# A fused decoder layer: first turn's last outputs after all of m, the query weights' high part on ScalarE, the last down products behind the first scores

## The reference, cut to what matters

```python
def attn(x, w_qkv, w_swiglu, w_out):            # x is a layernorm of the input, 8 x 256 x 512
    q, k, v = split(rms(x) @ w_qkv.T, 3)
    q, k = rms(q), rms(k)
    w = exp(k)
    kv_cum, w_cum = cumsum(w * v, 1), cumsum(w, 1)
    y = sigmoid(q) * (kv_cum / (w_cum + 1e-06))
    u, g = split(y @ w_swiglu.T, 2)              # 2 x 2048 columns
    return x + u * silu(g) @ w_out.T             # m = u * silu(g), "down" = m @ w_out.T
x = x + attn(layernorm(x), ...)
x = x + cross_attention(layernorm(x), ctx, mask, w_q, w_k, w_v, w_o, b_o)   # 32 heads of 16, 8 groups, causal
x = x + ffn(layernorm(x), ...)                   # 8 experts, top 2, and a shared one
```

## Time and profile before

| | us |
|---|---|
| median of 3 runs (1362.88 to 1364.53) | 1363.5 |
| the profiled execution | 1360.16 |
| its span, first to last instruction | 1358.4 |
| PE busy | 1298.8 (96%) |
| PEld busy | 1033.3 (76%) |
| DVE busy | 875.4 (64%) |
| ACT busy | 725.6 (53%) |
| POOL busy | 739.1 (54%) |

### The profile page before, as it was taken

The page is one execution under the profiler, slowest core; times in us unless marked ns, Lnnn a source line. Parts: engine busy times, 40 slices in busy tenths (PEclk is TensorE's granted clock), DMA queues, the critical chain, the costliest instruction groups (busy, mean ns, idle before and its releaser), DMA issues.

```text
span 1358.4 us, 23793 instructions
## 1 busy us (share of the span) xinstructions
PE 1298.8 (96%) x7988; PEld 1033.3 (76%) x7988; DVE 875.4 (64%) x2182; ACT 725.6 (53%) x1305; POOL 739.1 (54%) x722
## 2 busy tenths in 40 slices
PE   8999997999999999999989999999989999999994
PEld 6888776888888888888877777777767977666672
DVE  5888755444556744445658788778786586666661
ACT  4444444444345444434328777777775325777772
POOL 4557676456657754566556556445553113656562
PEclk9999998999999999999999999999999999999997
DMA  6000011111112111111220000000012914555553
GB/s 232 1 1 1 16 32 62 47 47 47 47 47 77 64 47 48 47 47 47 96 91 21 2 21 21 21 21 5 3 48 89 393 52 149 102 97 108 100 99 42
DMA packets 30152, 86.21 MB, mean 63 GB/s; under 512 B 2960, under 2 KB 7824, under 8 KB 28624
## 3 DMA queue, kind: packets, MB, share of 16 engines
q1 hardware_dynamic: 19856, 59.51, 12.4%
q0 software_dynamic: 10176, 25.17, 9.4%
HBM read 65.54 MB, written 19.14 MB: 62 GB/s over the span
## 4 chain that ended last, share of the span: by engine, by line
PE 76%; DVE 6%; POOL 6%; ACT 5%; issue 4%; DMA 1%; POOLq 0%; DVEq 0%; ACTq 0%
PE ps L974 12%; PE ps L976 11%; PE ps L975 11%; PE ps L1091 7%; PE ps L1093 6%; PE ps L1092 6%; PE ps L1249 5%; PE ps L1430 5%; PE ps L1241 2%; DVE den L1914 2%; ACT sc L1744 2%; PE ps L1341 2%; PE ps L1273 2%; PE ps L1267 1%; ACT pt L1732 1%
## 5 line engine op out<-in xcount | busy, mean ns | idle before, releaser
L770 POOL TENSOR_TENSOR w_up<-w_up_raw,w_up 128x512 fp32r<-128x512 f32 x120 | 134.2, 1162 | 89.2 <-ACT w_up L1575 89.2
L2088 DVE TENSOR_TENSOR acc<-ps,acc 128x512 f32<-128x512 f32 x128 | 88.0, 688 | 124.6 <-PE ps L976 123.9
L2219 DVE CUSTOM_DVE_ANT_0 sc<-ps,msk 128x256 f32<-128x256 f32 (+1 forms) x512 | 146.3, 353 | 26.6 <-PE ps L1241 15.2
L1732 ACT COPY pt<-ps 128x512 f32<-128x512 f32 x192 | 111.6, 581 | 77.4 <-PE ps L1249 77.4
L948 POOL DMA_INDIRECT out<-yx,ids x39 | 77.0, 1974 | 82.0 <-DMA out<-yx,ids 53.5
L1249 PEld LDWEIGHTS ps<-ident,sc 128*128 128x128 f32 x768 | 83.6, 140 | 45.0 <-issue 24.0
L1744 ACT ACTIVATE sc<-sc,mxs 128x256 f32<-128x256 f32 x256 | 116.8, 508 | 1.3 <-DVE mxs L2219 0.9
L866 POOL TENSOR_TENSOR sc<-mxs,sc 128x512 f32<-128x512 f32 x64 | 64.6, 1042 | 92.9 <-DVE mxs L2219 92.9
L1249 PE MATMUL ps<-ident,sc 128*128 128x128 f32 x768 | 109.7, 279 | 3.7 <-ACT pt L1732 3.7
L1091 PE MATMUL ps<-yt,w_up 128*128 128x512 f32 x256 | 99.9, 390 | 2.1 <-ACT ups__93 L1625 1.4
L974 PE MATMUL ps<-w_dn,m_s 128*128 128x512 f32 x256 | 99.7, 390 | 0.7 <-DVE acc L2088 0.7
(11 more groups left out here) (332 smaller groups left out, 3664.8 us busy)
## 6 DMA issues: line engine op xcount, KB each, us to landing
rawx<-weights SPq DMA_DIRECT2D x8, 1536.0 KB, 12.9
w_up_raw<-weights SPq DMA_DIRECT2D x15, 768.0 KB, 4.4
w_dn_raw<-weights SPq DMA_DIRECT2D x16, 512.0 KB, 5.3
wlow<-weights SPq DMA_DIRECT2D x3, 1536.0 KB, 6.4
ctx_raw<-ctx_t SPq DMA_DIRECT2D x8, 512.0 KB, 4.8
h_rows<-hd POOLq DMA_DIRECT2D x16, 256.0 KB, 4.8
out<-acc SPq DMA_DIRECT2D x4, 1024.0 KB, 4.7
w_up_raw<-weights SPq DMA_DIRECT2D x15, 256.0 KB, 4.7
```

The costliest lines, as they stand in the source:

```text
L770: ins = nc.gpsimd.tensor_tensor(out=to[:, j, 1, two, :, :].rearrange("p o k n -> p (o k n)"), in0=raw[:, j, 1, two, :].rearrange("p o n -> ...
L1732: nc.scalar.copy(pt[:, u % PLACES, :], bank).then_inc(turned[k], 1)
L2088: nc.vector.tensor_tensor(acc[:, tile, :], ps[:, BANK_D[t % 2], :], acc[:, tile, :], ALU.add).then_inc(mlp["acc"], 1)
L2219: ins = nc.vector.tensor_tensor_reduce(sc[:, at_, n * w:(n + 1) * w], ps[:, u % 4, n * w:(n + 1) * w], m_in, -0.25, 3e38, ALU.add, ALU.min ...
```

## The change

It touches three places. (1) In the first turn `y_a(7, 1)` goes from the middle of DVE's list to its end, behind both lows of chunk 1; low(0,0,0) goes ahead of the second up_2; in turn 1 PE's downs 0 and 1 go behind p6, together with the wait for y_a(7, 1). For this batch the denominators are made in place in `yraw`, whose place is free a little later than that of `wce_last` (wait for three steps of the first weights' split in place of one). (2) In turn 15 ACT makes the hi of the query weights, between silu_1 and p7_copy, in place of POOL; and POOL issues the zero rows in its turn 1, not ahead of `ctx_split(0)`. (3) Downs 6 and 7 of turn 15 go behind the scores of set 0, and down 5 behind the queries; DVE makes the mask and h_c of batch 1 ahead of reading the queries; DVE and PE both wait for the last down's sum behind it.

```diff
-        def wce_of(b):
-            return wce_last[:, :] if b + 1 == BATCH else wce[:, :]
+        def wce_of(b, half):
+            return yraw[:, b % PAIRED, half, :] if b + 1 == BATCH else wce[:, :]
+        def den_of(b, half):
+            return yraw[:, b % PAIRED, half, :] if b + 1 == BATCH else den[:, :]
...
 POOL, split_slot
-                own.link(nc.gpsimd.tensor_copy(wsplit[:, p, 0, :], wlow[:, p, 1, :]))
+                if name == "x":
+                    pool.wait_ge(c["x_hi"], 1)
+                else:
+                    own.link(nc.gpsimd.tensor_copy(wsplit[:, p, 0, :], wlow[:, p, 1, :]))
...
                 split_dn(u)
+                if u == 1:
+                    zero_rows()        # the two DMA issues of line 834, which go from behind this loop
...
 PE, turns 1 to 15
-                if u == 1:
-                    pe.wait_ge(a["y"], 2 * BATCH)
-                down(u - 1, 0)
+                if u > 1:
+                    down(u - 1, 0)
                 p7(u, 0)
                 p7(u, 1)
-                down(u - 1, 1)
+                if u > 1:
+                    down(u - 1, 1)
                 p6(u, 0)
                 p6(u, 1)
+                if u == 1:
+                    pe.wait_ge(a["y"], 2 * BATCH)
+                    down(0, 0)
+                    down(0, 1)
                 down(u - 1, 2)
...
 PE, behind values
-            for t in range(PIECES - 2):
+            for t in range(PIECES - 3):
                 down(TURNS - 1, t)
             pe.wait_ge(c["hT"], TPB)
             for half in range(2):
                 queries(half, ps[:, 2 + half, :])
-            for t in range(PIECES - 2, PIECES):
-                down(TURNS - 1, t)
+            down(TURNS - 1, PIECES - 3)
...
 PE, pass_c, behind scores(b, u // 4)
+                    if b == 0 and u == 0:
+                        down(TURNS - 1, PIECES - 2)
+                        down(TURNS - 1, PIECES - 1)
+                        pe.wait_ge(mlp["acc"], PIECES * TURNS)
...
 ACT, w_cum and the turns
-                    act.wait_ge(mlp["w_up"], 1)
-                nc.scalar.activation(wce_of(b), ps[:, 5, :], ACT.Copy, bias=1e-6).then_inc(a["wce"], 1)
+                    act.wait_ge(mlp["w_up"], 3)
+                nc.scalar.activation(wce_of(b, half), ps[:, 5, :], ACT.Copy, bias=1e-6).then_inc(a["wce"], 1)
...
+                if u + 1 == TURNS:
+                    act.wait_ge(raw_slot["x"], 32)
+                    nc.scalar.copy(wsplit[:, 0, 0, :], wlow[:, 0, 1, :]).then_inc(c["x_hi"], 1)
                 if u > 0:
                     p7_copy(u, 0)
...
 DVE, turn 0
             up_2(0, 0)
-            up_2(0, 1)
             up_1(0, 0)
             hidden_1(0, 0)
+            low(0, 0, 0)
+            up_2(0, 1)
             up_1(0, 1)
             hidden_1(0, 1)
-            low(0, 0, 0)
             low(0, 1, 0)
-            y_a(BATCH - 1, 1)
             hidden_2(0, 0)
             hidden_2(0, 1)
             low(0, 0, 1)
             low(0, 1, 1)
+            y_a(BATCH - 1, 1)
...
 DVE, behind values_read
-            for t in range(1, PIECES - 2):
-                sum_down(TURNS - 1, t)
-            for half in range(2):
-                queries_read(0, half, ps[:, 2 + half, :], c["first"])
-            for t in range(PIECES - 2, PIECES):
+            for t in range(1, PIECES - 3):
                 sum_down(TURNS - 1, t)
             masks(0)
             h_c(1, 0)
             h_c(1, 1)
-            dve.wait_ge(mlp["acc"], PIECES * TURNS)
+            for half in range(2):
+                queries_read(0, half, ps[:, 2 + half, :], c["first"])
+            sum_down(TURNS - 1, PIECES - 3)
...
 DVE, pass_c, behind the maxes of units 0 and 1
+                    if b == 0 and u == 0:
+                        sum_down(TURNS - 1, PIECES - 2)
+                        sum_down(TURNS - 1, PIECES - 1)
+                        dve.wait_ge(mlp["acc"], PIECES * TURNS)
```

More of the change, by code:

```diff
@@ L281, in decoder_layer @@
         den = at("den", [P, 2 * SEQ], F32)
-        wce_at = place[0]
         raw_j0 = at("raw_j0", [P, 4, 2 * P], F32)
-        wce_last = at("wce_last", [P, 2 * SEQ], F32, off=wce_at + 4 * D)
         ya_at = place[0]
@@ L433, in decoder_layer @@
         c = signals(
-            "c_", wo_hi="the output weights' hi", ones="v's columns of ones and zeros", half="the two masks of rows",
+            "c_", x_hi="slot of the queries' weights with hi", wo_hi="the output weights' hi", ones="v's columns of ones and zeros", half="the two masks of rows",
             ctx="contexts loaded, by 16", ctx_s="contexts split", mask_i="masks loaded, by 16", pad="masks of padding",
@@ L816, in _, with zero_rows @@
             chc = own
+            def zero_rows():
+                zeros = causal[:, 0:P].rearrange("p (o n) -> p o n", o=1).broadcast_to([P, D // P, P])
+                for rows in (h_rows, out):
+                    pool.dma_start(rows[BATCH * SEQ:ROWS, :].rearrange("p (o n) -> p o n", n=P), zeros).then_inc(d["zero"], 16)
             def rstd_c(b):
@@ L829, in _ @@
                 split_dn(u)
+                if u == 1:
+                    zero_rows()
                 if u + 1 == MLP_GROUPS:
                     second_rest()
-            zeros = causal[:, 0:P].rearrange("p (o n) -> p o n", o=1).broadcast_to([P, D // P, P])
-            for rows in (h_rows, out):
-                pool.dma_start(rows[BATCH * SEQ:ROWS, :].rearrange("p (o n) -> p o n", n=P), zeros).then_inc(d["zero"], 16)
             def ctx_split(b):
@@ L1184, in _ @@
                 p2(u, 1)
+                if u > 1:
+                    down(u - 1, 0)
+                p7(u, 0)
+                p7(u, 1)
+                if u > 1:
+                    down(u - 1, 1)
+                p6(u, 0)
+                p6(u, 1)
                 if u == 1:
                     pe.wait_ge(a["y"], 2 * BATCH)
-                down(u - 1, 0)
-                p7(u, 0)
-                p7(u, 1)
-                down(u - 1, 1)
-                p6(u, 0)
-                p6(u, 1)
+                    down(0, 0)
+                    down(0, 1)
                 down(u - 1, 2)
@@ L1910, in y_a @@
                 dve.wait_ge(a["wce"], s + 1)
-                nc.vector.scalar_tensor_tensor(out=den[:, :], in0=ps[:, 6, :], scalar=1.0, in1=wce_of(b), op0=ALU.add,
+                nc.vector.scalar_tensor_tensor(out=den_of(b, half), in0=ps[:, 6, :], scalar=1.0, in1=wce_of(b, half), op0=ALU.add,
                                                op1=ALU.mult).then_inc(a["den"], 1)
                 dve.wait_ge(a["den"], s + 1)
-                nc.vector.reciprocal(den[:, :], den[:, :]).then_inc(a["rec"], 1)
+                nc.vector.reciprocal(den_of(b, half), den_of(b, half)).then_inc(a["rec"], 1)
                 dve.wait_ge(a["rec"], s + 1)
@@ L1919, in y_a @@
                     dve.wait_ge(mlp["ws"], 2)
-                nc.vector.tensor_tensor(yraw[:, b % PAIRED, half, :], ps[:, 4, :], den[:, :], ALU.mult).then_inc(a["y"], 1)
+                nc.vector.tensor_tensor(yraw[:, b % PAIRED, half, :], ps[:, 4, :], den_of(b, half), ALU.mult).then_inc(a["y"], 1)
             def y_lo(b, half):
```

## The result

The changed kernel took 1352.1 us (median of 4 runs, 1350.05 to 1352.98) beside 1364.0 us for the kernel before (4 runs, 1362.88 to 1367.78): ratio 0.9913, 95% interval 0.9894 to 0.9931, so 9.4 to 14.5 us. The profiled execution took 1352.46 us, its span 1350.7 us.

A forecast was written before the change was run, and what follows sets the result against it. PE, busy for 96% of the span, was taken to bound the kernel, its stops being lost time. The terms 6.3 - 0.1 + 2.5 + 1.95 = 10.65 us took the median from 1363.5 to 1352.8 us, range 1350.5 to 1357.

The forecast's parts named there:

- Part 1: First turn: PE's 3.73 us stop ahead of p2 goes, 3.8 us, and its slow matmuls, 2.5 us; 0.1 us lost elsewhere.
- rival A: First turns: the clock falls anyway, from the two short stops together; gain 7.2 us, 1356.3; chance 0.08.
- the 5.25 us of all twelve: Turn 1: the time p2's twelve matmuls took, forecast to become 2.7 us if the clock stays up.
- The term of 2.5 us for the clock: Turn 1: saving on p2's twelve matmuls if the granted clock stays up.
- Part 2: Into attention: splitting the query weights sooner removes PE's 2.59 us stop but for a handover; 2.5 us.
- rival C: Turn 15: ACT's new wait for the query weights makes u2_copy late for p5; a 25 us landing gives 1365; chance 0.02.
- Part 3: Attention's start: downs behind the first scores cut the idle 2.81 us between score sets to 0.85; 1.95 us.
- one wait of 0.85 us: PE's wait for the last down's sum, between the scores of sets 0 and 1, left after the change.
- rival B: Attention's start: the wait for the last sum holds PE and the late downs gain nothing; gain 8.7 us, 1354.8; chance 0.07.
- for gains eaten by a place that I didn't look at I take 0.03: Whole kernel: chance 0.03 given to no change, for gains lost at a place not examined.

The follow-up runs named there:

- before_fill: Kernel before, with fourteen useless PE matmuls in the 3.73 us stop ahead of p2 of turn 1; 1363.5 us, ratio 0.9987.
- zero_back: Changed kernel, POOL's sums waiting for DVE's low part of T3, zero rows issued behind the turns' loop again; 1349.9 us, ratio 0.9884.
- xhi_back: Changed kernel, POOL's sums waiting for DVE's low part of T3, query weights' hi made by POOL again; 1351.5 us, ratio 0.9893.
- p3_only: Kernel before with only the last downs behind the first scores and mask and h_c earlier; 1363.0 us, ratio 0.9991.
- order_split: Changed kernel, POOL's sums waiting for DVE's low part of T3, PE's wait for the last down's sum cut in two; 1351.0 us, ratio 0.9884.
- after_timed: Changed kernel unchanged, timed again beside three kernels with POOL's extra wait; 1352.9 us, ratio 0.9907.
- p1_only: Kernel before with only the first turn's reordering (y_a(7, 1) behind both lows, downs 0 and 1 behind p6); 1361.6 us, ratio 0.9966.
- after_again: Changed kernel unchanged, run once more for a second profile; 1348.5 us (one run).
- before_again: Kernel before unchanged, run once more for a second profile; 1363.8 us.
- p2_only: Kernel before with only the query weights' hi made by ACT and zero rows issued in POOL's turn 1; 1360.6 us, ratio 0.9964.
- before_order: Kernel before, with POOL's sums at the change of halves waiting for DVE's low part of T3; 1361.6 us, ratio 0.998.

## Why the prediction was right, and where it was not

**Part 1** held where it was looked at. p2 starts at 225.19 (forecast 225.3), down(0,0) at 233.48 without a stop (233.5), and the clock stays, so rival A didn't happen. The gain was 6.32 (6.2). One reading was wrong: of the slow matmuls only the first took 0.79 us, the ones behind it 0.63. The sum doesn't rest on it, for it used the 5.25 us of all twelve. The term of 2.5 us for the clock was read from one execution. before_fill puts it at 1.3 to 2.4, and with it the whole part at 5.2 to 6.3.

**Part 2**: 2.75 us against 2.5. The working gave 2.8 us to the hi and 1.6 to the zero rows, for a stop of 2.59: zero_back shows that the hi alone removes the stop, xhi_back that the zero rows alone leave 0.82 us. ACT's copy took 2.76 us at 653.23 and nobody waited for it; rival C didn't come near.

**Part 3**: 1.98 us against 1.95, in the profile of p3_only. In the forecast one wait of 0.85 us was left; it measured 1.33. DVE's last sum, changed kernel:

```profile
699.45 0.69 DVE L2106 TENSOR_TENSOR acc<-ps,acc 128x512 f32<-128x512 f32 x1 [0.39 <-PE ps L984]
```

It ends at 700.14, and PE's transpose of h starts at 700.75: the handover takes 0.61 us, where the sum had 0.15 (702.75 to 702.9). That is 0.46 of the 0.48 us. The wait that rival B named is there, as order_split shows, but half a microsecond less of it isn't kept.

**The step that failed** is the one left out: "for gains eaten by a place that I didn't look at I take 0.03". I read the change of halves as covered, since PE is busy for all of the 200 us. It is covered only as long as DVE, not POOL, gets through; in four of five profiles with a full clock in the first turn and no extra wait of POOL, it didn't (the changed kernel, after_timed, p1_only, before_fill; not after_again). In none of the four with the stop and the low clock in the first turn (before, before_again, p2_only, p3_only) did it collide. Nine profiles are few for a rule, and why the first turn should matter 200 us later isn't shown. The forecast of the profiled execution, 1349.5, was therefore 3 us too low (1352.46), and after_again, which doesn't collide, came in at 1348.5.

**Why the median, forecast as 1352.8, still came out at 1352.1.** The medians differ by 11.9 us and the profiled spans by 7.7. Two things can make up the 4.2 us between them; neither is in the forecast, and no trace shows their shares, so that the median agrees with it to 0.7 us is in part luck.

The first is the low clock behind the 2.59 us stop ahead of keys, which cost 4.2 to 5.05 us where it came: of the six profiles that have the stop, in before_again and p1_only, not in before, before_order, before_fill and p3_only. The record has the mean granted clock of each timed execution. It was 0.988 or less in 23 of the 60 executions of the kernel before that were timed beside the experiments, all of them at 1365.2 us or more, and in 15 of the 48 of before_order, before_fill, p1_only and p3_only. It was so in none of the 9 of p2_only, which has the first turn's stop but not this one, and in none of the 31 of the changed kernel and its variants, which all have 0.991 or more. So the executions with the lowest clock go with this stop, and part 2 takes them away. In which stretch a timed execution lost its clock is not on record.

The second is a rival to it: the timed executions of the kernel before may collide too, though its two profiles don't, and then the change loses nothing to the collision. The profiled 1360.16 us and the collision's 3.85 make 1364.0, the median beside the result. before_order, in which POOL waits, has eight of 12 executions under 1362 us; the kernel before has five of 60. That speaks for it, but no trace of the kernel before shows a collision.

**Open**: what decides whether DVE gets in behind POOL's first sum or its fourth; how often the timed executions of the kernel before collide; why a 2.59 us stop lowers the clock at times.

## What to carry to other kernels

A change that takes away a stop also changes the executions in which the stop would have cost more than the profiled one shows; take two profiles of the kernel before before pricing a clock. Where POOL and DVE have long elementwise work on SBUF at once and PE waits for DVE's, order them by a wait: 0.45 us paid here against 3.85 us of risk. And an engine that is busy for 100% of a stretch says nothing of how near its feeder is to being late: read the slack of the operation that it waits for.

## What the runs showed of the hardware

- A DVE subtraction of 128x1024 with two inputs in SBUF took 1.22 us alone, and 3.33 or 7.03 to 7.05 us beside POOL's back-to-back sums. POOL's sums of 128x512 took 2.3 us where DVE got through and 1.3 us where it didn't: DVE was held up through one of POOL's instructions or through four, and which of the two differs between executions of one program.
- TensorE's granted clock fell in all five profiles with the first turn's stop of 3.68 to 3.73 us, in 2 of 6 with the 2.59 us stop (2.57 in one), in the four with the collision's stop of 2.9 us, and in none of the stops of 0.7 to 1.7 us that were looked at. The low clock behind the same stop cost 1.3 to 2.4 us and 4.2 to 5.05 us by place.
- Fourteen matmuls of no use in the 3.73 us stop kept the granted clock at 1.00 (before_fill, against 0.61 in the kernel before).
